# Attention layer 1 with 512 moving columns: values and row sums in column tiles, and the split of its weights shared with ScalarE

## The reference

```python
q = (query @ Wq).reshape(b, sq, 32, 16).transpose(0, 2, 1, 3)
k = (key @ Wk).reshape(b, sk, 8, 16).transpose(0, 2, 1, 3)
v = (value @ Wv).reshape(b, sk, 8, 16).transpose(0, 2, 1, 3)
k = jnp.repeat(k, 4, axis=1); v = jnp.repeat(v, 4, axis=1)
scores = jnp.einsum('bhqd,bhkd->bhqk', q, k) * 16 ** -0.5
out = jnp.einsum('bhqk,bhkd->bhqd', softmax(scores), v)
x = x + tanh(g_xattn[0]) * (out.transpose(0, 2, 1, 3).reshape(b, sq, 512) @ Wo)
```

## Time and profile before

| | |
|---|---|
| median of three runs | 2903.7 us |
| the profiled execution's own time | 2922.44 us |
| its span | 2920.6 us |
| mean granted TensorE clock | 0.978 of 2.4 GHz |
| PE busy | 2796.1 us (96%) |
| DVE, ACT, POOL busy | 1738.2, 1044.6, 826.1 us |

### The profile page before, as it was taken

One profiled execution on the slowest core, in us unless ns is written; L12 is line 12 of the kernel. 1 busy time (PEld: TensorE's weight loads), 2 busy tenths in 40 slices (PEclk: granted clock), 3 DMA queues, 4 the chain that ended last, 5 costly groups with the idle time before them and its releaser, 6 DMA issues.

```text
span 2920.6 us, 46999 instructions
## 1 busy us (share of the span) xinstructions
PE 2796.1 (96%) x14928; PEld 2352.5 (81%) x14928; DVE 1738.2 (60%) x3969; ACT 1044.6 (36%) x2823; POOL 826.1 (28%) x712
## 2 busy tenths in 40 slices
PE   7997899999999998888999999989999999999998
PEld 5885788888888887667888888878878888888886
DVE  6565645545545546666777777845552555555557
ACT  3441333333333333133444444421123444444442
POOL 5002324333432432323222222235533222212200
PEclk8799999999999999999999999999999999999999
DMA  4001101111111111111000110112111110000000
GB/s 144 12 1 64 36 27 54 36 36 43 40 43 32 47 36 30 37 30 37 30 29 29 29 29 29 30 40 58 58 48 37 30 27 26 26 27 26 28 6 30
DMA packets 59826, 106.35 MB, mean 36 GB/s; under 512 B 7184, under 2 KB 11536, under 8 KB 59536
## 3 DMA queue, kind: packets, MB, share of 16 engines
q1 hardware_dynamic: 56448, 96.49, 11.5%
q10 hardware_dynamic: 3216, 7.81, 0.7%
HBM read 100.09 MB, written 2.10 MB: 35 GB/s over the span
## 4 chain that ended last, share of the span: by engine, by line
PE 90%; DVE 6%; ACT 2%; issue 2%; POOL 0%; DMA 0%; ACTq 0%; DVEq 0%; POOLq 0%
PE four L583 51%; PE outp L583 23%; PE value L583 9%; PE turned L926 4%; PE turned L705 1%; DVE stats L1550 1%; DVE xt_lo L1579 1%; PE turned L630 0%; DVE nt L1522 0%; DVE nt L1524 0%; DVE probs L1574 0%; DVE x L1752 0%; DVE x L1958 0%; ACT sq L1302 0%; ACT vc L1199 0%
## 5 line engine op out<-in xcount | busy, mean ns | idle before, releaser
L556 POOL TENSOR_TENSOR w_hi<-raw,zero 128x512 fp32r<-128x512 f32 x352 | 375.1, 1066 | 1946.6 <-PE four L583 896.3
L1752 DVE SCALAR_TENSOR_TENSOR x<-outp,g_inv,x 128x512 f32<-128x512 f32 x768 | 556.6, 748 | 383.0 <-PE outp L583 382.6
L560 POOL TENSOR_TENSOR w_lo<-raw,w_hi 128x512 fp32r<-128x512 f32 x352 | 453.8, 1289 | 27.6
L583 PE MATMUL four<-xt_hi,w_lo 128*128 128x512 f32 x1024 | 425.2, 415 | 17.0 <-DVE xt_lo L1579 12.0
L583 PE MATMUL four<-xt_hi,w_hi 128*128 128x512 f32 x1024 | 407.0, 397 | 0.0
L583 PE MATMUL four<-xt_lo,w_hi 128*128 128x512 f32 x1024 | 404.4, 395 | 0.0
L583 PE MATMUL outp<-w_hi,a_lo 128*128 128x512 f32 x800 | 329.8, 412 | 14.4 <-DVE x L1752 7.6
L1199 ACT ACTIVATE pT<-turned 128x512 f32<-128x512 f32 x320 | 191.3, 598 | 361.5 <-PE turned L926 286.2
L583 PE MATMUL outp<-w_hi,a_hi 128*128 128x512 f32 x800 | 315.5, 394 | 0.0
L583 PE MATMUL outp<-w_lo,a_hi 128*128 128x512 f32 x800 | 314.8, 393 | 0.0
L1381 ACT ACTIVATE probs<-probs,top 128x128 f32<-128x128 f32 x512 | 199.6, 391 | 237.9 <-DVE top L1795 126.3
(11 more groups left out here) (257 smaller groups left out, 4644.6 us busy)
## 6 DMA issues: line engine op xcount, KB each, us to landing
raw<-in_stream SPq DMA_DIRECT2D x352, 256.0 KB, 2.6
ctx_raw<-in_ctx_t ACTq DMA_DIRECT2D x4, 512.0 KB, 5.8
x<-in_x_in ACTq DMA_DIRECT2D x2, 1024.0 KB, 11.8
kz<-kT SPq DMA_DIRECT2D x32, 64.0 KB, 2.3
pb<-in_position_bias ACTq DMA_DIRECT2D x1, 2048.0 KB, 8.6
out<-x SPq DMA_DIRECT2D x8, 256.0 KB, 2.0
qw<-in_qweight ACTq DMA_DIRECT2D x1, 768.0 KB, 4.0
ln_w<-in_ln_weight ACTq DMA_DIRECT2D x1, 256.0 KB, 2.7
```

The source lines that it names most:

```text
L556: pool.tensor_tensor(w_hi[:, k, :], raw[:, k % RAW, :], zero[:, :].to_broadcast([P, D]), ALU.add)\
L560: pool.tensor_tensor(w_lo[:, k, :], raw[:, k % RAW, :], f32(w_hi[:, k, :]), ALU.subtract)\
L583: m = pe.matmul(out_, l, r, start=start, stop=stop, skip_group_check=True)
L1752: dve.scalar_tensor_tensor(out=x[:, b, :], in0=O[no_f(k) % 2][:, :], scalar=scale, in1=x[:, b, :], op0=ALU.mult, op1=ALU.add)\
```

## The change

- `values` now holds the values (`vv`, 32 columns wide, with zeros beside the 16 features) as weights and moves the probabilities, 512 columns (four heads) at once, in four column tiles of 32 output rows. One call covers four key heads. A second call with a matrix of ones (`ones_by_half`) in the place of the values gives the row sums, already spread over the 16 rows of each head. Each batch has two halves, accumulated in one bank each.
- The result comes out with features on rows, so `attended_turn` is gone. The features stand in another order, and the rows of Wo are loaded in that order: 32 DMAs of 16 rows (`load_outputs`) take the place of four.
- `normed` now takes the reciprocal of all 512 columns of the sums (L1652 of the changed kernel) and multiplies once per batch.
- `shifted` subtracts over 768 columns; the last 256 columns of each unit go through ACT straight from PSUM, as two exponentials with the negated maximum as bias (`direct`). The exponential of the rest covers 768 columns. `scores` waits for `direct` too.
- `pT` has six buffers in the place of two.
- Clearing: DVE clears half of `kz`, POOL the other half after its second chunk; `vv` and `ones_by_half` are cleared after `ct_lo`. `shifted(0)` waits for all copies of the keys.
- ACT makes the high parts of chunks 2 to 6.
- `output` and the steps after it come one step later or more; the loop has 41 steps in the place of 38.

```diff
@@ SyncE @@
+            def load_outputs(j):
+                c = CHUNK_AT[("L0", ("o", j))]
+                first = CHUNK_AT[("L0", ("o", 0))]
+                sp.wait_ge(w_done, c - RAW + 1)
+                for no in range(PARTS):
+                    hh, cg = no // 4, no % 4
+                    row, src = 32 * cg + 16 * hh, 64 * (cg % 2) + 16 * j
+                    sp.dma_start(raw[row:row + 16, c % RAW, :], stream[first + 2 * hh + cg // 2, src:src + 16, :])\
+                        .then_inc(raw_in[c % RAW], 16)
...
-            sp.wait_ge(AS[0]["cleared"], 1)
+            sp.wait_ge(AS[0]["cleared"], 3)
...
+            for j in range(4):
+                load_outputs(j)
@@ GpSimd @@
             for k in range(RING):
-                split(k, 16 * (k // RAW + 1), k + 1)
+                split(k, raw_count(k), k + 1, k in HI_BY_ACT)
+                if k == 1:
+                    pool.memset(A0["kz"][:, 2:4, :, :], 0.0).then_inc(AS[0]["cleared"], 1)
@@ TensorE @@
                     if u:
                         pe.wait_ge(s["sub"], u)
+                        pe.wait_ge(s["direct"], u)
...
+                def values(b, hh, sums):
+                    pe.wait_ge(s["pT"], 8 * b + 4 * hh + 4)
+                    if hh == 0 and b:
+                        pe.wait_ge(s["normed"], b)
+                    if hh == 0 and not b:
                         pe.wait_ge(s["j_out"], 12)
+                    for cg in range(4):
+                        kv = 4 * hh + cg
+                        w = buf["ones"][:, hh, :] if sums else buf["vv"][:, b, kv, :]
+                        m = mm((V, O[1])[sums][32 * cg:32 * cg + 32, :], w, buf["pT"][:, (8 * b + kv) % 6, :],
+                               hh == 0, hh == 1)
...
+                    u, r = k - 2, k % 4
+                    if 0 <= u < L.UNITS:
+                        turn(2 * u)
+                    if r in (0, 2) and 4 <= k <= L.UNITS + 2:
+                        values((k - 4) // 4, r // 2, 0)
+                    if r in (1, 3) and 9 <= k:
+                        output((k - 9) // 4, r // 2)
+                    if 0 <= u < L.UNITS:
+                        turn(2 * u + 1)
+                    if r in (0, 2) and 4 <= k <= L.UNITS + 2:
+                        values((k - 4) // 4, r // 2, 1)
@@ ScalarE @@
+                weights_hi(2)
                 for t in range(2):
                     act.wait_ge(s["proj"], t + 1)
                     copy(buf["vT"][:, half(t)], J[t]).then_inc(s["j_out"], 1)
+                weights_hi(3)
...
                 for r in range(4):
+                    if r < 3:
+                        weights_hi(4 + r)
                     c = CHUNK_AT[("L0", ("k", r))]
...
+                    if k < L.UNITS:
+                        act.wait_ge(s["top"], k + 1)
+                        for e in range(2):
+                            o = act.activation(buf["pr"][:, k % 3, (6 + e) * P:(7 + e) * P],
+                                               four[:, 3, e * P:(e + 1) * P], ACT.Exp,
+                                               bias=buf["top"][:, k % 2, 6 + e:7 + e], scale=1.0)
+                        o.then_inc(s["direct"], 1)
...
-                        p = buf["pr"][:, k % 3, :]
-                        act.activation(p, p, ACT.Exp).then_inc(s["exp"], 1)
+                        cols = buf["pr"][:, k % 3, 0:6 * P]
+                        act.activation(cols, cols, ACT.Exp).then_inc(s["exp"], 1)
@@ VectorE @@
+                    dve.tensor_reduce(top_, src, AX_X, ALU.max, negate=True).then_inc(s["top"], 1)
+                    dve.wait_ge(s["top"], u + 1)
+                    dve.tensor_tensor(buf["pr"][:, u % 3, 0:6 * P].rearrange("p (a e t) -> p a e t", a=3, e=2),
+                                      src[:, 0:3], top_[:, 0:3].unsqueeze(3).to_broadcast([P, 3, 2, P]), ALU.add)\
                         .then_inc(s["sub"], 1)
...
+                def normed(b):
+                    dve.wait_ge(s["values"], 2 * b + 2)
+                    then(dve.reciprocal(buf["an"][:, :], O[1][:, :]))
+                    dve.tensor_tensor(buf["an"][:, :], V[:, :], buf["an"][:, :], ALU.mult).then_inc(s["normed"], 1)
...
-                    if k >= 4 and k % 4 in (0, 2) and (k - 4) // 4 < B:
-                        normed((k - 4) // 4, k % 4 // 2)
+                    if k >= 6 and k % 4 == 2 and (k - 6) // 4 < B:
+                        normed((k - 6) // 4)
```

More of the change, by code:

```diff
@@ L350, in build @@
                 "kz": sb("kz", [P, 4, B, 2 * P], F32, st),
[L351 to L358, removed]
+                "vv": sb("vv", [P, B, 8, 32], F32, st),
+                "ones": sb("ones_by_half", [P, 2, 32], F32, st),
                 "top": sb("top0", [P, 2, 8], F32, st),
-                "inv": sb("inv0", [P, 2, 16], F32, st),
             }
@@ L461, in build @@
         AS = [
-            sems("_L0", "proj j_out vt v_rows wk cleared scores tiny sub exp turned pT values normed a_turned "
+            sems("_L0", "proj j_out vt v_rows wk cleared scores top tiny sub direct exp turned pT values normed "
                         "a_hi a_lo outp x_acc"),
@@ L476, in build @@
         SETUP = 4
+        HI_BY_ACT = range(2, 7)
         KEY_LAG = 3
@@ L502, in half, with raw_count @@
             return slice(t * HALF, (t + 1) * HALF)
+        def raw_count(c):
+            return sum(16 * (PARTS if STREAM[n][0] == "L0" and STREAM[n][1][0] == "o" else 1)
+                       for n in range(c % RAW, c + 1, RAW))
         def newton_base(layer, what):
@@ L708, in turn @@
                     m.then_inc(s["turned"], 1)
[L710 to L717, removed]
-                        pe.wait_ge(s["j_out"], 12)
[L719 to L723, removed]
-                            told(m)
[L725 to L734, removed]
+                def values(b, hh, sums):
[3 more added lines that the diff above has]
+                    if hh == 0 and not b:
+                        pe.wait_ge(s["j_out"], 12)
+                    for cg in range(4):
[3 more added lines that the diff above has]
+                               hh == 0, hh == 1)
+                        if cg < 3:
+                            told(m)
+                    if sums:
+                        m.then_inc(s["values"], 1)
                 def output(b, part):
@@ L741, in output @@
                         pe.wait_ge(w_done, CHUNK_AT[("L0", ("o", 3))] + 1)
-                    for c in (2 * part, 2 * part + 1):
-                        m = mm3(O[0][:, :], (buf["a_hi"][:, tokens(c)], buf["a_lo"][:, tokens(c)]),
-                                ring(CHUNK_AT[("L0", ("o", c))]), c == 0, c == KT - 1, last=c == KT - 1)
+                        if b:
+                            pe.wait_ge(s["x_acc"], b)
+                    for j in (2 * part, 2 * part + 1):
+                        a = buf["a_hi"][:, tokens(j)], buf["a_lo"][:, tokens(j)]
+                        m = mm3(O[0][:, :], a, ring(CHUNK_AT[("L0", ("o", j))]), j == 0, j == KT - 1,
+                                last=j == KT - 1)
                         if b == B - 1:
@@ L1626, in narrow_heads @@
                                       ALU.subtract).then_inc(ctx_done, 1)
+                dve.memset(buf["vv"][:, :, :, :], 0.0).then_inc(s["cleared"], 1)
+                then(dve.memset(buf["ones"][:, :, :], 0.0))
+                for hh in range(2):
+                    then(dve.memset(buf["ones"][:, hh, 16 * hh:16 * hh + 16], 1.0))
                 norm_stats(0)
```

110 lines of the change are left out of this document (52 added, 58 removed).

## The result

The changed kernel takes **2931.65 us** (median of four runs, 2928.13 to 2932.26). The kernel before, run beside it, takes 2902.88 us (2899.48 to 2908.96). The ratio is 1.0077, with a 95% interval of 1.0043 to 1.0111: slower by 0.8%. The forecast was 2920 us with a range of 2884 to 2934.

What follows compares the result with a forecast made beforehand. PE bounds the loop, then DVE's chain with the reciprocal makes PE wait. Start +0.5 and +2.3, scores(2) to (10) -19.7, five batches -1.3, end +3.9 give 2908; clock falls +12 give 2920 us, range 2884 to 2934.

Steps and rivals of the forecast that it cites:

- The choice between profile and median: Loop's 0.50-clock stretch, 18.3 us, taken as mostly absent from timed executions; the kernel before stands 18 us below its profile.
- slow in itself: Rival: timed executions had the same slow stretch; both kernels 18.7 lower, 2901 with falls, 2889 without; chance 0.17.
- Column tiles: Value matmuls on PE: four column tiles run side by side, 1.0 us a call.
- serial rival: Column tiles run one after another: 3.5 us a call, nearly 10 more per batch, some 2985; chance 0.07.
- The reciprocal: DVE's reciprocal of 512 columns in `normed` takes 3.35 us.
- The new wait: PE's scores wait for DVE's subtraction behind `normed`: 3.2 us per batch, seven times.
- The batch at full clock: Loop over units: a batch takes 16.8 us in place of 17.05.
- The start: Ahead of scores(2): +0.5 for clearing and high parts (between -3 and +2), +2.3 for steps 0 and 1.
- two direct stalls: Steps 0 and 1: scores wait for direct exponentials behind the second late query copy, 1.15 us twice, +2.3.
- The end: From scores(30) to the last output: 28.7 us against 24.8, or +3.9.
- The clock: TensorE's clock falls behind most of the seven waits: 3.41 us stretches cost 1.7 each, +12; double length +24.
- The cheap reciprocal: Rival: 512 columns cost 0.7 us, the wait is 0.5, a batch 14.1, total 2887, not slower; chance 0.17.

Runs made afterwards that it cites:

- e2b_filled: From the changed kernel, twelve unread 128x512 matmuls for PE ahead of the second turn, in the 7 steps in which PE waits: 2914.89 us.
- before_again: The kernel before, unchanged, profiled once more: 2908.59 us.
- e3_halves: From the changed kernel, reciprocal cut into two 256-column halves, the second behind the next unit's subtraction, a_hi and a_lo one step later: 2913.34 us.
- e1_copy: From the changed kernel, the reciprocal of the 128x512 row sums replaced by a copy of the same size on the same engine: 2896.57 us.
- e11_best: From e3_halves: sums ahead of values, reciprocal cut 320/192, direct exponentials from unit 2, chunk 6's high part later, last batch in halves: 2890.49 us.
- e6_old_start: From the changed kernel, the start undone: VectorE alone clears the keys, GpSimd makes all high parts: 2937.29 us.

## Why the prediction was right, and where its steps were off

The sum of the prediction was 2908 at full clock, which puts the start of the last output, output(7), at 67.85 + 2.8 + 29.7 + 84.0 + 28.7 = 213.05 us. It started at 235.16, 22.1 later. With 0.5 more up to the next stage and 1.5 in the later ones this makes 2932.2, the profiled 2932.26. The lines of the changed kernel behind these numbers, and the same place in e2b_filled, which has no slow stretch there:

```profile
69.02 0.71 PE L608 MATMUL four<-kz,qT 32*128 32x256 f32 x8 [1.29 <-ACT shifted L1306]
...
203.15 0.71 PE L608 MATMUL four<-kz,qT 32*128 32x256 f32 x8
...
213.40 0.77 PE L608 MATMUL four<-ct_hi,w_lo 128*128 128x512 f32 x1 [3.33 <-issue]
...
235.16 0.77 PE L608 MATMUL outp<-w_hi,a_lo 128*128 128x512 f32 x1 [4.75 <-DVE x L1686]
```

```profile
190.10 0.71 PE L609 MATMUL four<-kz,qT 32*128 32x256 f32 x8
...
220.55 0.76 PE L609 MATMUL outp<-w_hi,a_lo 128*128 128x512 f32 x1 [4.74 <-DVE x L1691]
```

Step by step:

- **The choice between profile and median: right.** The first profile's slow stretch was its own (before_again). Of 55 further executions of the kernel before, timed beside the experiments, 51 took 2897.4 to 2909.1 us and four 2917 to 2921. These four were not profiled; their times fit a stretch like the first profile's, which would then be rare and not unique. The rival "slow in itself" falls.
- **Column tiles: right.** A call takes 1.0 us, and the serial rival is out.
- **The reciprocal: right.** 3.358 us against 3.35. Over 192, 256, 320 and 512 columns it took 1.35, 1.75, 2.15 and 3.36: 6.3 ns per column. The Trainium skill's repeat count of 8 ("VectorE: DVE Perf Modes", "First, the fixed hardware budget") had given an estimate of 4.3 us for 512. The measurement decides; by an estimate at the page's 0.96 GHz it is six cycles per column.
- **The new wait: right in place and size**, 3.48 us against 3.2. It comes six times ahead of scores (3.89 us the first time) and a seventh time, 3.33 us long, ahead of the early piece of the next stage.
- **The batch at full clock: 17.47 us (e2b_filled), not 16.8.** An even step takes 3.81, not 3.6: a turn ahead of a value call lasts 0.58, where I took the 0.49 of the turns before the short matmuls. The DVE-bound step from the sums to the next scores is 6.61 in place of 6.4. So even at full clock the changed kernel's batch is 0.4 us longer than the 17.05 of before, where the prediction had it 0.25 shorter. With the part from scores(2) to scores(10) (31.1 in e2b_filled against 29.7) this is some 4.7 us.
- **The start: right within 1.6 us.** The two direct stalls cost 2.7, forecast 2.3. Scores(2) started at 69.02 against a forecast 70.65.
- **The end: 1.8 us too low.** The forecast was 28.7 at full clock. The changed kernel took 32.01, and of these 1.5 are the clock: the early piece behind the seventh wait takes 4.36 us (213.40 to 217.76) and in e3_halves, at full clock, 2.83. That leaves 30.5, and e2b_filled took 30.45 (190.10 to 220.55). Two terms are missing from the sum: PE waits 0.69 us for the last `pT`, and the last output waits for the addition to x, 0.74 us, which stands behind `a_lo` on DVE. e3_halves took only 28.3, because its first half reciprocal cuts the wait of 3.33 us to 1.13.
- **The clock: the term that was too small.** The prediction took seven stretches of the shortest length seen, 3.41 us at 1.7 us each, for +12, and named double length for +24. The stretches in the loop are 6.83 us. They cost 2.8 each in the five batches (20.24 less 17.47, or 13.9 together) and 1.8 ahead of scores(10); the one behind the seventh wait is 3.42 us long and costs 1.5: 17.2 in all. I had taken the shortest stretch in the trace, behind an idle time unlike this one. The double length stood as the other bound, +24, and the range held the result for that reason. It had to cover more than the clock: the prices at full clock were too low by 6.5 us as well, against 1.6 gained at the start, and beyond the double lengths the range left 2 us for them. That all of it fitted under 2934 is in part luck.
- **The cheap reciprocal: a rival priced too well.** e1_copy gave it the price of a copy and measured 2896.57. With 0.69 us left for the first pass (the price forecast for that rival, 0.7) a wait of 0.81 stays, and the batch is 14.80 rather than 14.1. Against the kernel before it was to gain 16.7 us and gained 7: the sign was right, the size less than half.

Together: +4.7 in the loop and +1.8 at the end for prices, -1.6 for the start, +17.2 for the clock give 22.1. Against the kernel before without its stray slow stretch (before_again), the stage compares like this, in us:

| part | before_again | changed | difference |
|---|---|---|---|
| start of scores(2) | 67.17 | 69.02 | +1.9 |
| scores(2) to scores(10) | 31.01 | 32.92 | +1.9 |
| scores(10) to scores(30) | 85.23 | 101.21 | +16.0 |
| scores(30) to the last output | 24.82 | 32.01 | +7.2 |

Of these 26.9 us the half clock makes 17.2. The largest part of the rest is the end, 5.7 us at full clock: there a wait for DVE's chain comes twice, 3.33 us ahead of the early piece and 4.75 ahead of the last output. The column tiles did what they were to do: on PE alone a batch would be 14.1 us (two steps of 3.81, two of 3.25). DVE's chain took that back and 0.4 more per batch, and the half clock then charged PE's idle time a second time.

## What to carry to other kernels

When one engine is made faster, work out the chain that now closes the loop on the other engines, with the new long instruction in it. Ask what stands ready behind it: here finished scores lay 3.4 us behind a reciprocal that nobody needed so soon. Cutting the long instruction in two with the urgent work between was worth 18 us; making its input earlier, and mending the start and the end, another 23, with no arithmetic removed. On TensorE count an idle time twice if it is long enough to bring the clock down; several short waits can be much cheaper than one long wait of the same sum.

## What the runs showed of the hardware that I had not expected

- More work made the kernel faster: about 2.8 us of unread matmuls per batch took 17 us off the total, because the granted clock stayed at 1.00.
- In the loop of e3_halves a wait of 1.29 us in each batch brought a slow stretch after two of five waits. The waits of 0.63 to 0.82 us in e1_copy and e11_best brought none, nor did one of 1.04; one of 1.22 in e1_copy did. The waits of 3.48 us and more did so every time: for 6.83 us all six times in the changed kernel, but for 3.4 us two times out of six in e6_old_start.
- GpSimd's power takes 160 ns per column (128x512 in 81.9 us); its subtraction of the same size takes 1.28 us in that run.
- Each change between logarithm and exponential cost ScalarE a load of 1.28 us.
